# A gated weight mean as a tensor-scalar with per-partition operands, and four of twelve weight pieces rounded by ScalarE

## The reference

```
x   = x + tanh(g_xattn) * scan_block(ctx, layernorm(x))
x   = x + tanh(g_ffn)   * mlp(layernorm(x))

scan_block:  u  = silu(conv(in_proj(ctx)));  B, C, dt = projections of u
             state = state * exp(dt * A) + (dt * u) * B      # 16 states, step by step
             y  = (sum over states of state * C + D * u) * silu(z)

weight_quant(w):  scale = 1 / clip(mean(|w|), 1e-5)
                  clip(round(w * scale), -1, 1) / scale
mlp:         h = silu(bitlinear(x, w1)) * bitlinear(x, w2);  bitlinear(h, w3)
             # bitlinear: rmsnorm, 8-bit activations, quantised weight
```

## Time and profile before

| | us |
|---|---|
| three runs | 718.25, 718.27, 718.80 |
| median | 718.27 |
| profiled execution, its own time | 717.76 |
| span of its instructions | 716.0 |
| POOL busy | 625.4 (87%) |
| DVE busy | 605.9 (85%) |
| ACT busy | 515.4 (72%) |
| PE busy | 512.1 (72%) |
| mean granted clock of TensorE | 0.889 of full speed |

### The profile page before, as it was taken

The page is one execution under the profiler, slowest core; times in us unless marked ns, Lnnn a source line. Parts: engine busy times, 40 slices in busy tenths (PEclk is TensorE's granted clock), DMA queues, the critical chain, the costliest instruction groups (busy, mean ns, idle before and its releaser), DMA issues.

```text
span 716.0 us, 8124 instructions
## 1 busy us (share of the span) xinstructions
PE 512.1 (72%) x2562; PEld 314.2 (44%) x2562; DVE 605.9 (85%) x839; ACT 515.4 (72%) x971; POOL 625.4 (87%) x300
## 2 busy tenths in 40 slices
PE   9787889556451758787575668578686876758897
PEld 3243434223441435555353435345453544445554
DVE  7679778977999898988868888999889889888865
ACT  5844866159867868868677777898788797677653
POOL 1499999979999999999999999988998899988431
PEclk9999999969556998999785979899999998989999
DMA  4695875258950000037310000027510000000001
GB/s 169 217 402 209 305 293 211 89 181 333 413 238 15 6 29 2 29 125 266 125 61 19 31 0 16 1 82 250 197 70 6 15 2 16 0 16 16 1 16 44
DMA packets 23930, 80.78 MB, mean 113 GB/s; under 512 B 2432, under 2 KB 4608, under 8 KB 20816
## 3 DMA queue, kind: packets, MB, share of 16 engines
q1 hardware_dynamic: 23888, 80.27, 30.7%
HBM read 72.53 MB, written 7.73 MB: 112 GB/s over the span
## 4 chain that ended last, share of the span: by engine, by line
DVE 29%; ACT 21%; PE 21%; POOL 13%; issue 11%; DMA 3%; SPq 1%; DVEq 0%; ACTq 0%; POOLq 0%
DVE hh L738 7%; ACT da L708 5%; DVE hh L735 4%; POOL hh L686 4%; POOL hh L757 4%; PE bank_y L787 3%; PE bank_a L936 3%; PE bank_t L1080 3%; DMA wq<-x 2%; PE bank_b L942 2%; POOL hh L680 2%; POOL hh L752 2%; ACT room L1091 2%; DVE sm L640 2%; ACT room L977 2%
## 5 line engine op out<-in xcount | busy, mean ns | idle before, releaser
L738 DVE TENSOR_TENSOR_SCAN hh<-da,hh 128x1024 f32<-128x1024 f32 x96 | 217.5, 2277 | 6.7 <-POOL hh L686 3.5
L787 PE MATMUL bank_y<-ident,hh 128*128 128x128 f32 x1024 | 146.4, 293 | 25.0 <-POOL hh L757 19.3
L757 POOL TENSOR_TENSOR hh<-hh,cc 128x1024 f32<-128x1024 f32 x64 | 160.3, 2505 | 2.4 <-DVE hh L738 2.4
L787 PEld LDWEIGHTS bank_y<-ident,hh 128*128 128x128 f32 x1024 | 130.0, 152 | 54.9 <-POOL hh L757 27.9
L752 POOL TENSOR_TENSOR hh<-hh,cc 128x1024 f32<-128x1024 f32 x64 | 151.3, 2364 | 3.1 <-ACT hl L721 2.0
L686 POOL TENSOR_TENSOR hh<-pair,bb 128x1024 f32<-128x1024 f32 x30 | 71.6, 2388 | 26.0 <-DMA bb<-xd_scratch 25.8
L735 DVE TENSOR_TENSOR_SCAN hh<-da,hl,hh 128x256 f32<-128x256 f32 x128 | 85.0, 728 | 0.0
L680 POOL TENSOR_TENSOR hh<-wq,bb 128x1024 f32<-128x1024 f32 x32 | 75.6, 2361 | 10.7 <-PE bank_y L787 10.7
L686 POOL TENSOR_TENSOR hh<-wq,bb 128x1024 f32<-128x1024 f32 x32 | 76.6, 2395 | 3.4 <-PE bank_y L787 3.4
L680 POOL TENSOR_TENSOR hh<-pair,bb 128x1024 f32<-128x1024 f32 x32 | 75.6, 2363 | 3.4 <-PE bank_y L787 3.4
L302 PE MATMUL bank_b<-room 128*128 128x512 f32 x96 | 47.4, 640 | 24.8 <-DVE wq L406 23.2
(11 more groups left out here) (250 smaller groups left out, 1046.5 us busy)
## 6 DMA issues: line engine op xcount, KB each, us to landing
bb<-xd_scratch SPq DMA_DIRECT2D x32, 512.0 KB, 5.2
cc<-xd_scratch SPq DMA_DIRECT2D x32, 512.0 KB, 7.7
wq<-weights SPq DMA_DIRECT2D x12, 1024.0 KB, 6.5
stage<-weights SPq DMA_DIRECT2D x8, 1024.0 KB, 6.7
xin<-x SPq DMA_DIRECT2D x4, 1024.0 KB, 5.5
room<-weights SPq DMA_DIRECT2D x4, 1024.0 KB, 9.8
u_scratch<-wq SPq DMA_DIRECT2D x6, 512.0 KB, 3.4
wq<-x SPq DMA_DIRECT2D x2, 1024.0 KB, 18.5
```

Source lines behind the costliest of these rows:

```text
L738: ins = v.tensor_tensor_scan(h, flat(dbank[k % 2]), h, 0.0, ALU.mult, ALU.add)
L757: ins = g_.tensor_tensor(hh[k % NH][:, :, :], hh[k % NH][:, :, :], cc[:, s * GN:(s + 1) * GN, :], ALU.mult)
L787: mm = pe.matmul(bank_y[:, (first + c) * P:(first + c + 1) * P], flat(hh[k % NH])[:, at:at + P], ident[:, :], start=False, stop=(s == STEP ...
```

## The change

Two places change. In `weight_mean` the product `g3d` was a scalar-tensor-tensor instruction that streams two operands (the mean, times the constant 1/127, times the gate); it becomes a tensor-scalar instruction that streams the mean and takes the gate as a scalar per partition and 1/127 as a constant. The result is the same product.

And pieces 1, 4, 7 and 10 are rounded by ACT in place of DVE, in the same slot, by an activation with function Identity, scale `winv` and bias MAGIC, both per partition. It waits for the load of the piece and for the means (mark "gx", which stands behind the reciprocals). The sign of these pieces now waits for ACT's own semaphore. No DMA is added, moved or removed.

```diff
-            WV.did(v.scalar_tensor_tensor(out=g3d, in0=wmean[:, 2:3], scalar=1.0 / 127.0, in1=gates[:, 1:2],
-                                          op0=ALU.mult, op1=ALU.mult))
+            WV.did(v.tensor_scalar(g3d, wmean[:, 2:3], gates[:, 1:2], 1.0 / 127.0, ALU.mult, ALU.mult))
...
+        def rounded_by_scalar(i):
+            return i in (1, 4, 7, 10)
+
+        def weight_round_scalar(act, i):
+            s = stage[round_stage(i)]
+            act.wait_ge(*d_stage[round_stage(i)].of(("round", i)))
+            act.wait_ge(*WV.of("gx"))
+            WA.did(act.activation(s, s, ACT.Identity, bias=magic, scale=winv[:, i // 4:i // 4 + 1]), ("round", i))
+
         def weight_sign(act, i):
-            act.wait_ge(*WV.of(("round", i)))
+            act.wait_ge(*(WA if rounded_by_scalar(i) else WV).of(("round", i)))
...
                         if k == sum_slot(i) and i % 2 == 0:
                             weight_sum(act, i)
+                        if k == round_slot(i) and rounded_by_scalar(i):
+                            weight_round_scalar(act, i)
                         if k == sign_slot(i):
                             weight_sign(act, i)
...
-                        if k == round_slot(i):
+                        if k == round_slot(i) and not rounded_by_scalar(i):
                             weight_round(v, i)
```

## The result

The changed kernel takes 719.14 us (median of 20 runs, 718.39 to 720.59) against 718.26 us for the kernel before on the same chip (20 runs, 716.17 to 720.56): ratio 1.0017, 95% interval 1.0009 to 1.0024. The forecast was 709.1 us. The profiled execution took 719.75 us with a span of 717.8.

The account below looks back on a forecast made before the run. POOL and DVE were taken as the candidates, with POOL full but for 5.19 us of idle time. That plus 3.96 us from four rounds made 9.15 us, giving 709.1 us; own range 707 to 711, full range 704.3 to 714.5.

Parts of the forecast that it names:

- part 1: Line 640 in the new form falls from 14.55 to 0.20 us; POOL's two idle times go, 5.19 us.
- Part 2: Four rounds leave DVE: 10.9 us less for DVE, and 0.99 us each, 3.96 us in all, saved on POOL.
- the upper bound: Most that DVE's chain could gain by 267 us, with none of ACT's rounds on it: 24.8 us.
- Part 3: Four rounds reach ACT at 2.10 us each, 8.4 us in all, covered by ACT's idle time and three slots of lead.
- Part 4: SP's order: piece 3's load is issued 2.1 us later in its slot; ACT's wait for data 0, bound 2 us.
- The sum: POOL gains 2.42 + 2.77 + 3.96 = 9.15 us and DVE's chain gains as much by 267 us: 709.1 us.
- The second: Rival: the starvation moves to line 581, two SBUF operands beside a running POOL; 714.3 us, 723.7 at full price; chance 0.06.
- The first: Rival: ACT becomes the bound for part of the stretch, with all four rounds on the chain; 712.3 us; chance 0.11.
- The third: Rival: line 640 keeps its duration in the new form; 714.3 us, or 722.7 if ACT's rounds stand in the chain; chance 0.05.
- The fourth: Rival: DVE's chain was the bound beyond 267 us, so its 13.9 us earlier start gets through; 704.4 us; chance 0.08.

Follow-up runs that it names:

- the rounds alone: The changed kernel with the old two-operand form of line 640, four rounds still on ScalarE: 715.36 us, ratio 0.9963 to the kernel before.
- The same program: The changed kernel with eight rounds on ScalarE (all but pieces 0, 3, 6 and 9) and GpSimd's one stop in slot 20: six executions, 707.47 to 721.14 us.

## Why the prediction was wrong, step by step

**The reading of line 640 was right.** It waited for the ports, it took 0.20 us in the new form as forecast, the next scan started at 130.82 (forecast 130.20), and its stall cost 5.2 us: the kernel before with one stop of GpSimd gives just that back. One count was off: six boundaries between products passed line 640, not seven; the seventh was where GpSimd ran dry. It changes no term.

**The step that failed is in part 1: "POOL's two idle times go: 5.19 us on POOL."** It asked only whether line 640 would still wait, and not who asks for the ports next. That was the round of piece 0, two rows further down in the earlier trace rows, at 1.26 us. It was that short after the stall in front of it had let GpSimd run dry: GpSimd's next product started 0.16 us after it. The other rounds were let in at the next boundary, and each came a few products (at most four) behind a held-up product or an idle time. I took "a round is let in and costs GpSimd 0.99 us" as a property of the instruction, while it hung on what GpSimd had done before; taking away the first stall took away that cover. The stall then lasted longer (17.20 us for 14.55), and GpSimd's idle times grew from 5.3 to 11.7 us. Where VectorE makes no such request (all rounds on ScalarE), or GpSimd stops once beside it, the wait is gone: 709.51 and 708.60 us.

The Trainium skill ("SBUF — State Buffer", "Who interferes with whom") says in the lines next to the one that I used that a tensor-scalar in a two-port mode contends with GpSimd, that whoever comes first holds the ports for the whole instruction, and that the form with an accumulator does not contend. The first and the third agree with the runs (17.20 and 1.26 us against 2.32 us in every place). By the second the round would have waited for one product, some 2.3 us, and the forecast would have held; it passed six boundaries. I had seen that disagreement at line 640 and still priced the rounds by the rule.

**Part 2** was right where there is no stall: the four rounds cost GpSimd 4.02 us (forecast 3.96), and 5.6 us of the medians. On VectorE the four of before add up to 11.3 us, not 10.9, since that of piece 4 took 2.97; it bears on the upper bound alone. **Part 3** was right in its size, 2.08 to 2.09 us (forecast 2.10), and in its cover with one stop, where GpSimd idles 0.15 us. Behind the stall it was incomplete: the rounds alone brought 2.7 us by the ratio of 0.9963, some 4 in the faster group of executions and under 1 in the group that was profiled. **Part 4:** no round of ScalarE waited for a load in the changed kernel, as forecast.

**The sum** was right for a kernel without the stall. Forecast 709.1 us; 708.60 and 709.09 with a stop. The 709.51 with all rounds on ScalarE lies as near by chance, since other terms make it up. With the stop in slot 20 GpSimd's 120th product starts at 320.60 us rather than 328.87, and the profiled execution is 8.4 us shorter than the one before (709.37 for 717.76): what was gained by 250 us passes on to the end, as forecast. The medians are 9.9 us apart, since the profiled execution with the stop was the slowest of its four (707.22 to 709.37).

**The rivals.** The second named the mechanism, a starvation that moves, and put it at line 581, because it looked only among instructions with two operands. Line 581 took 1.75 us in the changed kernel, which the small instruction behind it explains. The first, ScalarE as the bound, is real at twelve rounds; at four it is seen only behind a stall. The third is refuted by the 0.20 us. The fourth gave 704.4 us for a larger gain; that was reached only with rounds that need no port (702.03), for another reason.

## What to carry to other kernels

Before you count a stall as gained, list the instructions behind it that need the same resource and ask whether they were short only because the stall had emptied the other engine. Where GpSimd runs such products without a gap, a VectorE instruction like this tensor-scalar in its fast form, or like the product of two operands in SBUF, can wait until GpSimd runs dry; a stop of 0.15 us in GpSimd's program right there (708.60 for 719.14 us), or a form that needs no shared port, took it away here. When an edit brings nothing, look for the same length of stall one or two rows further down.

## What the runs showed of the hardware that was not expected

- An instruction of VectorE can be kept out for 17.20 us, over six boundaries between products of GpSimd that follow each other without a gap; and a stop of GpSimd of 0.10 or 0.15 us at the request or one product before it was enough to let it in.
- A fast round (1.25 us) that gets in holds up the product beside it by 1.0 us. The same tensor-scalar with an accumulator takes 2.32 us and holds up nothing, but the kernel with it no longer gives the reference's result.
- Written in views of 23x89 columns or of every second column, a tensor-scalar kept its fast form, with the same wait: 1.26 us at the least with every second column, 1.55 with 23x89, against 2.32 for the form with an accumulator.
- The same program ran from 707.5 to 721.1 us from one execution to the next. In the one that was profiled, the slowest, a round was kept out; that it was let in in the fast ones fits their times and was not seen.
